# An expert stage: weights fetched in runs of 1 KB, two fetches on ScalarE's queue, an earlier split, and the last rows in a free buffer

## The reference, cut to what matters

```python
xf = x.reshape(B * T, D)                      # 4096 rows of 256
logits = xf @ gate_W.T
pi = _sinkhorn(-logits)                       # 20 iterations
_, top_idx = jax.lax.top_k(pi, 2)
g = jnp.einsum('nd,efd->enf', xf, W_gate)     # 8 experts, F = 1024
u = jnp.einsum('nd,efd->enf', xf, W_up)
y = jnp.einsum('enf,edf->end', jax.nn.silu(g) * u, W_down)
for k in range(2):
    out = out + y[top_idx[:, k], n_ar] * pi[:, k:k + 1]
```

## Time and profile before

| | |
|---|---|
| median of 3 runs | 2167.04 us (2166.58 to 2167.49) |
| the profiled execution | 2164.73 us |
| its span | 2163.1 us |
| PE busy | 1915.4 us (89%) |
| DVE busy | 1331.6 us (62%) |
| ACT busy | 1385.9 us (64%) |
| POOL busy | 703.1 us (33%) |
| mean granted clock of PE | 0.937 |
| bytes moved by DMA | 276.08 MB |

### The profile page before, as it was taken

How to read it: one execution, slowest core, us unless ns; L and a number is a source line. 1 busy time by engine, 2 the same in 40 slices (tenths; PEclk the granted TensorE clock), 3 DMA queues, 4 the chain that set the end, 5 groups by cost and what they waited for, 6 DMA issues and landing times.

```text
span 2163.1 us, 37845 instructions
## 1 busy us (share of the span) xinstructions
PE 1915.4 (89%) x11671; PEld 1090.0 (50%) x11671; DVE 1331.6 (62%) x2221; ACT 1385.9 (64%) x1586; POOL 703.1 (33%) x697
## 2 busy tenths in 40 slices
PE   6999999999945579998998989976989999999998
PEld 5722333333332468887887878865722222222255
DVE  4511144445667545555465555427689999999967
ACT  5699999999832233233233233224799999999944
POOL 2000111111110212121222122111068888888932
PEclk9999999999955689999999999987999999999999
DMA  5744333444100644554544554529944426354021
GB/s 195 243 97 69 59 77 76 83 88 88 40 31 17 246 161 144 200 180 143 199 167 154 191 186 140 187 91 333 315 106 90 103 43 133 59 139 67 9 87 69
DMA packets 131072, 276.08 MB, mean 128 GB/s; under 512 B 18588, under 2 KB 69022, under 8 KB 129656
## 3 DMA queue, kind: packets, MB, share of 16 engines
q1 hardware_dynamic: 117160, 228.72, 38.2%
q10 hardware_dynamic: 6736, 22.94, 3.1%
q0 software_dynamic: 6960, 21.77, 3.0%
HBM read 365.58 MB, written 96.21 MB: 213 GB/s over the span
## 4 chain that ended last, share of the span: by engine, by line
PE 46%; ACT 21%; DVE 13%; DMA 7%; issue 7%; POOL 3%; DVEq 1%; ACTq 1%; SPq 1%; POOLq 0%
PE psum L2654 16%; PE psum L1345 12%; PE psum L1326 9%; ACT A1f_probs L1370 8%; ACT A1f_probs L1378 8%; DMA hidden<-e_squares 4%; PE psum L381 3%; DVE e_w_low L2575 2%; ACT e_w_high L2463 2%; DMA e_turned<-hidden 2%; POOL A1f_probs L1547 2%; PE psum L850 1%; DVE e_hT L2558 1%; PE psum L396 1%; ACTq L2351 1%
## 5 line engine op out<-in xcount | busy, mean ns | idle before, releaser
L1326 PE MATMUL psum<-A_qa,A_ka 50*128 50x512 f32 x2048 | 408.3, 467 | 23.5 <-DVE A_qa L1413 6.2
L1326 PEld LDWEIGHTS psum<-A_qa,A_ka 50*128 50x128 f32 x2048 | 176.4, 185 | 470.5 <-DVE A1f_probs L1423 243.4
L2654 PE MATMUL psum<-e_w_high,e_xT 128*128 x1136 | 389.5, 406 | 22.0 <-DVE e_xT L2548 20.2
L1547 POOL TENSOR_TENSOR A1f_probs<-A1f_probs,A1f_bias 128x512 f32<-128x512 f32 x256 | 327.1, 1288 | 81.4 <-ACT A1f_probs L1378 81.0
L1423 DVE SCALAR_TENSOR_TENSOR A1f_probs<-psum,A1f_bias 128x1024 f32<-128x1024 f32 x256 | 311.6, 1217 | 23.5 <-PE psum L1326 19.7
L1378 ACT ACTIVATE A0f_probs<-psum 128x1024 f32<-128x1024 f32 x256 | 315.5, 1232 | 0.0
L1366 ACT ACTIVATE A0f_probs<-psum 128x1024 f32<-128x1024 f32 x256 | 313.2, 1224 | 2.7 <-PE psum L1326 2.7
L2654 PE MATMUL psum<-e_w_high,e_hT 128*128 x1136 | 236.8, 301 | 59.6 <-DVE e_hT L2558 59.6
L1345 PE MATMUL psum<-A1f_probs,v 128*32 128x512 f32 x2048 | 274.0, 606 | 17.2 <-POOL A1f_probs L1547 16.2
L1370 ACT ACTIVATE A1f_probs<-A1f_probs 128x1024 f32<-128x1024 f32 x256 | 274.0, 1070 | 4.5 <-DVE A1f_probs L1423 3.5
L1345 PE MATMUL psum<-A0f_probs,v 128*32 128x512 f32 x2048 | 273.8, 607 | 0.0
(11 more groups left out here) (297 smaller groups left out, 2506.3 us busy)
## 6 DMA issues: line engine op xcount, KB each, us to landing
e_w_raw<-in_experts ACTq DMA_DIRECT2D x67, 3072.0 KB
hidden<-e_squares SPq DMA_DIRECT2D x69, 512.0 KB
e_turned<-hidden SPq DMA_DIRECT2D x276, 128.0 KB
qk_parts<-L_part SPq DMA_DIRECT2D x64, 512.0 KB, 4.1
A_qa<-qk_parts SPq DMA_DIRECT2D x192, 128.0 KB, 4.2
A_ka<-qk_parts SPq DMA_DIRECT2D x192, 128.0 KB, 6.3
om<-results SPq DMA_DIRECT2D x16, 512.0 KB, 6.9
e_w_raw<-in_experts SPq DMA_DIRECT2D x2, 3072.0 KB
```

The lines of the kernel that those rows point to most:

```text
L1326: mm = e.matmul(ps[:, side * HALF:(side + 1) * HALF], self.qk.ka[rows, s, pair, kt * P:(kt + 1) * P].bitcast(FP32R), self.qk.qa[rows, s, p ...
L1547: e.tensor_tensor(fourth, fourth, self.bias_of(*w[1:], slice(self.FOURTH, GH)).rearrange("p h q -> p (h q)"), ALU.mult).then_inc(self.mult ...
L2654: mm = e.matmul(out, left[part].bitcast(FP32R), moving.bitcast(FP32R), start=start and i == 0, stop=stop and i == 2)
```

## The change

```diff
-WEIGHT_RUN = 4096
+WEIGHT_RUN = 1024
...
-    REST = 4
+    REST = 2
+    LAST = MOE_TILES - 1
...
     def fetch(self, e, buf, row, j, sem):
         e.dma_start(self.w.raw[:, buf, :],
-                    self.w.weights[bass.ds(self.planned(e, row, j), 1), :, :].rearrange("e p n -> p (e n)")
-                    ).then_inc(sem, DMA)
+                    self.w.weights[bass.ds(self.planned(e, row, j), 1), :, :].rearrange("e p n -> p (e n)"),
+                    max_dma_last_dim=WEIGHT_RUN).then_inc(sem, DMA)
 
     def sync(self, e, mirror_stored, beside):
...
         beside(e, (2, 3))
-        self.fetch(e, 1, THIRD, 0, self.weights_in)
         for j in range(self.BY_PE):
...
-        e.wait_ge(self.h_low, self.BY_PE)
+        e.wait_ge(self.downed, self.BY_PE + 1)
         beside(e, (0, 1))
...
     def pool(self, e):
-        def fetch_fourth(k):
-            with self.if_second(e, k):
-                e.wait_ge(self.low_ready, self.low_value("second", k))
-                self.fetch(e, 0, FOURTH, 0, self.fourth_in)
...
     def act(self, e):
...
         def split_hidden(j):
             self.wait_turned(e, j)
-            if j:
-                e.wait_ge(self.downed, j)
+            if j == self.BY_PE:
+                e.wait_ge(self.h_low, j)
+            elif j:
+                e.wait_ge(self.downed, self.hT_free(j))
...
             e.activation(self.hid[:, :], self.GU[:, 0, :], ACT.Silu).then_inc(self.silu, 1)
-            if self.LAG < j < MOE_TILES - 1:
+            if j == 0:
+                e.wait_ge(self.first_low, 3)
+                self.fetch(e, 1, THIRD, 0, self.weights_in)
+            if j == self.REST:
+                e.wait_ge(self.low_ready, self.low_value("second", self.REST))
+                self.fetch(e, 0, FOURTH, 0, self.fourth_in)
+            if self.LAG < j < self.LAST:
                 fetch_fourth(j - self.LAG)
-            if j >= 1:
+            if 1 <= j < self.LAST:
                 e.wait_ge(self.upped, j)
                 high_part(j, 0, DOWN_AT)
+            if j == self.LAST:
+                split_hidden(self.BY_PE)
...
+        split_hidden(self.LAST)
         for j in range(self.BY_PE, MOE_TILES):
-            split_hidden(j)
             move_y(j)
...
+    def hT_free(self, j):
+
+        return self.BY_PE if j == self.LAST else j
+
+    def hT_of(self, j, part):
+
+        return self.turned[:, part, :].rearrange("p (f n) -> p f n", f=FC) if j == self.BY_PE else self.hT[:, part, :, :]
...
     def dve(self, e, beside):
...
+            if j == self.LAST:
+                rest_of_hidden(self.BY_PE)
             multiply(j)
...
-        low_part(MOE_TILES - 1, "up", DC * F, DOWN_AT)
-        low_part(MOE_TILES - 2, "down", DOWN_AT, WIDE)
-        for j in range(self.BY_PE, MOE_TILES):
-            rest_of_hidden(j)
+        low_part(self.LAST - 1, "down", DOWN_AT, WIDE)
+        rest_of_hidden(self.LAST)
...
     def pe(self, e):
...
-        down(MOE_TILES - self.LAG)
-        turn_hidden(MOE_TILES - 1)
-        down(MOE_TILES - 1)
+        turn_hidden(self.LAST)
+        down(self.BY_PE)
+        down(self.LAST)
```

More of the change, by code:

```diff
@@ L2357, in high_value @@
         for k in range(1, MOE_TILES):
-            order += [("second", k)] * (k < self.REST) + [("up", k)] + [("down", k - 1)] * (k > 1)
+            order += [("second", k)] * (k < self.REST) + [("up", k)] * (k < self.LAST)
+            order += [("down", k - 1)] * (k > 1)
             order += [("second", k + 1)] * (k + 1 == self.REST)
@@ L2367, in low_value @@
             order += [("second", k)] * (k < self.REST) + [("down", k - self.LAG)] * (k > self.LAG)
-            order += [("up", k - 1)] * (k > 1) + [("gate", k)]
+            order += [("up", k - 1)] * (k > 1) + [("gate", k)] * (k < self.LAST)
             order += [("second", k + 1)] * (k + 1 == self.REST)
-        order += [("up", MOE_TILES - 1), ("down", MOE_TILES - 2)]
+        order += [("down", self.LAST - 1)]
         return order.index((kind, j)) + 1
@@ L2446, in pool @@
         for j in range(MOE_TILES):
-            if 1 <= j < self.REST:
-                fetch_fourth(j)
             if j + ROW_BUFS < MOE_TILES:
@@ L2452, in pool @@
                 self.store_y(e, j - self.LAG)
-            if j + 1 == self.REST:
-                fetch_fourth(self.REST)
         for j in range(MOE_TILES - self.LAG, MOE_TILES):
@@ L2528, in wait_turned @@
             e.wait_ge(self.h_turned, j - self.BY_PE + 1)
+    def hT_free(self, j):
+        return self.BY_PE if j == self.LAST else j
+    def hT_of(self, j, part):
+        return self.turned[:, part, :].rearrange("p (f n) -> p f n", f=FC) if j == self.BY_PE else self.hT[:, part, :, :]
     def parts_of_hidden(self, j, part):
-        out = self.hT[:, part, :, :].bitcast(FP32R)
+        out = self.hT_of(j, part).bitcast(FP32R)
         if j >= self.BY_PE:
@@ L2551, in rest_of_hidden @@
             low, whole = self.parts_of_hidden(j, 1)
-            high = self.hT[:, 0, :, :]
+            high = self.hT_of(j, 0)
             high = high.rearrange("p f n -> p (f n)") if j >= self.BY_PE else high.rearrange(
@@ L2555, in rest_of_hidden @@
             e.wait_ge(self.h_high, j + 1)
-            if j:
-                e.wait_ge(self.downed, j)
+            if j and j != self.BY_PE:
+                e.wait_ge(self.downed, self.hT_free(j))
             e.tensor_tensor(low, whole, high, ALU.subtract).then_inc(self.h_low, 1)
@@ L2697, in down @@
             for f in range(FC):
-                mm = product(j, self.Y, (self.hT[:, 0, f, :], self.hT[:, 1, f, :]), DOWN_AT + f * D, D, f == 0,
+                mm = product(j, self.Y, (self.hT_of(j, 0)[:, f, :], self.hT_of(j, 1)[:, f, :]), DOWN_AT + f * D, D, f == 0,
                              f == FC - 1)
```

## The result

The changed kernel takes **2141.28 us** (median of 4, 2141.04 to 2143.76) against 2167.26 us for the kernel before on the same chip: ratio 0.9875, 95% interval 0.9853 to 0.9897. It is faster by 26 us, where 58 were forecast; the time lies in the range that was given (2099 to 2160). The profiled execution took 2141.04 us, its span is 2139.2 us, 23.9 less than before.

A forecast was written before the change was run, and what follows sets the result against it. TensorE, busy 89% of the span, was taken as the bound. Handovers -36, start-up -13 and end -9 sum to -58 us: 2106.7 from the profiled 2164.73, 2109 on the median's scale; range 2099 to 2160.

The forecast's parts named there:

- Runs of 1 KB at the handovers: At seven expert-buffer refills, smaller pieces let the store of squares land sooner, ending TensorE's stops; -36 of 37.8 us lost.
- The last rival: At the handovers, the wait goes by bytes, so 1 KB runs change nothing; 2145 us, no chance of its own.
- the half case: Queues share less than one for one, or the loads of `e_turned` suffer; 2132 us, chance 15%.
- the sharing one for one: In the DMA queues, after first waiting for pieces already taken up, a newcomer alternates with the fetch piece for piece.
- the load of `e_turned`: At the handovers, the load behind the store now shares with the fetch; 0.5 us counted as new.
- Start-up: First tiles of the expert stage, up to tile 7's gate product: -13 us, bounds -8 to -16.
- the early split: At start-up, second expert split in tile one: TensorE's second stop, 9.60 us, goes; the first stays.
- the third expert from ACT: At start-up, tile 0's store lands near 744.5, 3.5 us sooner, which the split of the second expert takes.
- Fourth expert from ACT: Early tiles: fetch issued near 754 instead of POOL's 785; tile 2's store lands 4.4 us later, hidden.
- The end: Last down products run without a stop, -9.8 us; next stage's loads cross the last scatters, +1; -9 in all.
- The slower rival: At the handovers, the store of squares lands later than now; with 5 us each, 2185 us; chance 8%.
- the generator: SP's store cannot be turned into pieces before ACT's whole fetch has been; 2152 us, 2154 for the median; chance 27%.

The follow-up runs named there:

- Experiment 3: Changed kernel with a different run length at each of the seven handovers, 512 B to 24 KB; 2140.70 us.
- experiment 2: Changed kernel with the refill at the seven handovers never fetched, so its output differs; 2106.57 us.
- experiment 7: Changed kernel with the second expert split in tile 3 again instead of tile one; 2152.04 us.
- experiment 6: Changed kernel with the third expert fetched by SP again, ahead of the first stores of squares, instead of by ACT; 2144.99 us.
- experiment 1: Changed kernel with runs of 4 KB instead of 1 KB in all fetches; 2150.57 us, ratio 0.9887 to the kernel before.
- experiment 8: Changed kernel with the last two tiles turned, split and multiplied in the old order; 2149.87 us.
- experiment 10: Kernel of experiment 5 with each piece cut in two halves, the second issued only after the tile's squares; 2281.39 us, ratio 1.0524.
- experiment 4: Changed kernel fetching only the first 0.5 to 2.5 MB of each refill in 1 KB runs, so its output differs; 2118.55 us.
- experiment 5: Changed kernel with each refill fetched in three 1 MB pieces, one, two and three tiles behind the handover; 2122.00 us, ratio 0.9785.

## Why the prediction was wrong in size and right in sign

**Runs of 1 KB at the handovers: forecast -36, measured -1.9** (-4.5 with the average of the five profiles). This is the step that failed: "so a newcomer first waits for pieces already taken up, 261/16 = 16 per DMA engine". The earlier trace rows held 261 pieces and 1.07 MB, and fit 16 pieces and 67 KB alike, since all pieces there were of one size; I priced the pieces. Experiment 3 shows 64 to 2457 packets waited for, and 1.2 to 1.6 MB in 3.7 to 4.3 us each time. The wait was to fall to 0.8 us and did not fall, so the stops stayed, and with them the lower clock. The row that was meant to tell the two apart, 333 pieces from 3.25 to 4.25 us, covers one microsecond and bounds the wait from below only: it can't say that 76 KB would not have been waited for had so much been taken up. The last rival, "if the wait behind a fetch goes by bytes, not by pieces", is what happened, in so far as pieces don't count; it gave 2145 and should have had a chance of its own, not a share of the half case. What was right there: the place, the prize (36 us by experiment 2), the sharing one for one, and the load of `e_turned`, which was counted at 0.5 us and takes 0.53 more on average.

**Start-up: forecast -13, measured -16.** Taken back one at a time, the early split is worth 12.8 us (experiment 7; 13 in the prediction: a stop of 9.6, a product at full clock, small stops), the third expert from ACT 3.6 to 4.6 (experiment 6; forecast 3.5, covered by the split), 1 KB runs 2.7 (experiment 1). They overlap, since a later store hides the split. The first stop shrank by 1.5 us, which the forecast had left unchanged. The rule of the Trainium skill, "DMA: Bandwidth & Descriptors", section "Issuing engines are not separate DMA queues", which lets a second issuer save sequencer time only, does not describe this case: the same bytes, issued by ACT, let SP's store land 3.6 to 4.5 us sooner (experiment 6). The other half of its statement, that all DMAs run on the same 16 engines and interleave, is what 865 to 866 us shows, where q1, q0 and q10 share them with 60.7, 24.6 and 19.3%.

**Fourth expert from ACT: nothing**, as forecast. Tile 2's store is issued at 756.85 and its load at 764.93, 8.1 us, forecast 4.4 and still in time.

**The end: forecast -9, measured -9.5 + 2.1.** The products run as predicted. The loads of the next stage that cross the last scatters cost 1.1 us in the results' DMA (3.52 against 2.41 before and 2.40 in experiment 8), as forecast. The other 1.0 is POOL's wait, which the prediction did not have and whose cause is open.

**The slower rival and the generator** are refuted: no distance at a handover of the changed kernel is above 9.31 us, and 512 B runs are no slower than 1 KB runs at the same places.

**The range.** Its lower end, 2099, is called the sum of all upper bounds. These are 37.8, 16 and 10 us, which gives 2101 in the profiled execution and 2103 for the median; it does not matter for the outcome.

## What to carry to other kernels

A short transfer that the critical path waits for suffers from a bulk fetch under way by what stands ahead of it, here up to 1.2 MB or some 4 us, so look when each is issued and how many bytes come at a time. Cutting the bulk in smaller descriptors did little (2 to 13 us at the handovers by the profiles); cutting it in DMAs of 1 MB, in three tiles in place of one, gave 14 to 20 us here. When all pieces in a row are of one size, a count and a sum of bytes are the same evidence: before pricing a change of size, look for a row with another size, or let the two readings be two rivals with a chance each. And a wait that is put into an engine's stream only to time a DMA holds up everything behind it on that engine, in every tile: in experiment 10 it cost more than the stops that it was to remove.

## What the runs showed of the hardware

- While a fetch of one queue is under way, a newcomer on another queue waits 3.7 to 4.3 us, in which 75 to 78 KB move for each of 16 engines at runs of 512 B to 4 KB, 80 at 8 KB, 96 at 24 KB (experiment 3, and the changed kernel for 1 KB); with 0.5 or 1 MB fetched it is what is left of that (experiment 4). I had read it as 16 descriptors.
- A short DMA behind a bulk one on its own queue fares worse than behind one on the other queue: 16.19 us from the store to its load, with 9.73 us in the store's issue, against 11.70 to 12.63 (experiment 6).
- A load of 1 KB pieces is itself held up longer when the fetch beside it has 1 KB runs: its first 3 us moved 0.15 MB, and 0.33 beside 4 KB runs.
- Of the tiles two behind a handover, those of up to 11.76 us had a granted clock of 1.00 and 9.1 us of matmuls; those from 12.13 us on had 0.76 to 0.88 on average, and 10.1 to 11.5 us of matmuls, in place of 8.6. It is not the length of the tile that decides: tiles in which weights are split, of 12.78 to 13.25 us, kept 1.00 (the changed kernel and experiment 5).
- A conditional DMA that fetches nothing takes ACT about 0.46 us (three in a row start 0.46 us apart and take 1.0 us in all, 905.34 to 906.36 in experiment 10), and at that size it is hidden: the tiles of experiment 5 stay at 8.6 us.
